# Moving every matmul's two operands to fixed addresses modulo 256 bytes in an AdaLN block with an oscillator scan

## The chip, the cores and the metric

One core of a Trainium2 chip runs the whole program. The metric is device time in microseconds (us), the median of several executions. TensorE (PE in the profile) multiplies, VectorE (DVE), ScalarE (ACT) and GpSimd (POOL) compute beside it, and SyncE issues the transfers. Each of the 128 partitions of the on-chip memory (SBUF) holds the rows of many buffers one behind another; "address" below means the byte offset inside a partition.

## What is computed

Input `x` is [4, 2048, 512] in fp32, with one conditioning row of 512 for each of the four sequences.

```python
mod = silu(c) @ wmod                       # sa, ca, ga, sb, cb, gb
h = layernorm(x) * (1 + ca) + sa
omega, zeta, F = softplus(h @ W_omega), sigmoid(h @ W_zeta), h @ W_B
xs = scan over t of a damped oscillator (64 states z, 64 states y)
x = x + ga * (xs @ C.T + h @ D.T)
h = layernorm(x) * (1 + cb) + sb
xr, xk = mixes of h[t] and h[t-1] by mu_r, mu_k
x = x + gb * sigmoid(xr @ Wr.T) * (relu(xk @ Wk.T)**2 @ Wv.T)
```

## The kernel before

The 8192 rows are worked on as 16 chunks of 512 rows (first layer norm, projections, scan) and 32 units of 256 rows (everything behind the scan). Every fp32 matrix product is made of three float32r products: each operand is split into a high and a low part, and hi·hi, hi·lo and lo·hi are summed in PSUM. `product` (line 328 in the profile) issues them: for each of three passes and each slice `k` of 128 rows of the contraction, `pe.matmul(out, act[a][k], weight[w][k])`. The first operand is the standing one (128 columns, loaded into the array by a LDWEIGHTS, shown as PEld), the second is the moving one (256 or 512 columns). In the profile the moving one is named first: `ps_kr<-wr_hi,mix_r_hi` streams `wr_hi` past a standing `mix_r_hi`. The load for the next matmul runs while the present one streams.

The products of a unit, in this text under one letter each:

- **K** (`k_product`): `mix_k` moves (256 columns), `wk` stands, 48 matmuls, into `ps_kr`
- **R** (`r_product`): `wr` moves (512 columns), `mix_r` stands, 24 matmuls, into `ps_kr`
- **V** (`v_product`): `wv` moves (512), `kk_hi`/`kk_lo` stand, 24 matmuls, into `ps_tv`
- **H** (`h_part`): `wd` moves (512), `h` stands, 24 matmuls, into `ps_cd`
- **S** (`states_part`): `wc` moves (512), `xs_hi`/`xs_lo` stand, 6 matmuls, into `ps_cd`
- **P** (`projections`, once for each chunk): `h` moves (512), `proj` stands, 24 matmuls, into `ps_pt`
- **T1, T2** (lines 336 and 369): transposes of `x_in` and `xn2`, 16 for a chunk and 8 for a unit, `ident` moves (128 columns)

TensorE's order is written out by hand. In the steady part two units make one period: K T2 P R H S V, then K T2 H S T1 R T1 V. Every engine is a queue of its own with semaphores between them. After the residual add, `statistics2` on ScalarE squares both tiles of the unit (`squares`, line 582) and keeps only the row sums; the squares themselves go to a scratch buffer `square_out2` in bf16, and each square waits until the one two before it is done.

Buffers are taken one behind another, each at the next multiple of 32, the first of them at address 1152. Their addresses modulo 256, before and after, as the two lists of `sb(...)` give them:

| product | moving, before | standing, before | moving − standing | moving, after | standing, after | moving − standing |
|---|---|---|---|---|---|---|
| K | mix_k 64 | wk 128 | −64 | 192 | 0 | −64 |
| R | wr 128 | mix_r 64 | +64 | 0 | 64 | −64 |
| V | wv 128 | kk_hi, kk_lo 64 | +64 | 0 | 64 | −64 |
| H | wd 128 | h 128 | 0 | 0 | 64 | −64 |
| S | wc 128 | xs_hi, xs_lo 224 | −96 | 0 | 64 | −64 |
| P | h 128 | proj 128 | 0 | 64 | 128 | −64 |
| T1 | ident 128 | x_in 192 | −64 | 64 | 64 | 0 |
| T2 | ident 128 | xn2 64 | +64 | 64 | 64 | 0 |

All slices of a buffer that a matmul takes start a multiple of 512 bytes from the buffer's start, so a product has the same difference in all its matmuls. (−64 is taken modulo 256, +192 is the same.) Before, `gate_a` and `gate_b` lie at 160, `square_out1` at 96, `xs` at 224; the other large buffers lie at multiples of 64.

Of the kernel before, what the change touches and what calls it, by code (L numbers as in the profile page):

```python
# [7 lines left out]
F32 = mybir.dt.float32  # L8
F32R = mybir.dt.float32r
# [3 lines left out]
B, T, D, M = 4, 2048, 512, 64  # L13
P = 128
KC = D // P
CHUNK, UNIT, HALF = 512, 256, 256
# [3 lines left out]
TPU, TPC = UNIT // P, CHUNK // P  # L20
# [18 lines left out]
def build(nc, d):  # L39
    ctx = ExitStack()  # L40
    with ctx:
        def sb(name, shape, dt=F32):
            return ctx.enter_context(nc.sbuf_tensor(name, shape, dt))

        def sem(name):
            return ctx.enter_context(nc.semaphore(name))


        proj = [sb(f"proj_{n}", [P, KC, 256], F32R) for n in ("hi", "lo")]
        wd = [sb(f"wd_{n}", [P, KC, D], F32R) for n in ("hi", "lo")]  # L50
        wc = [sb(f"wc_{n}", [P, D], F32R) for n in ("hi", "lo")]
        wk = [sb(f"wk_{n}", [P, KC, D], F32R) for n in ("hi", "lo")]
        wr = [sb(f"wr_{n}", [P, KC, D], F32R) for n in ("hi", "lo")]
        wv = [sb(f"wv_{n}", [P, KC, D], F32R) for n in ("hi", "lo")]
        ident = sb("ident", [P, P])
        scan_bias = sb("scan_bias", [P, 4])
        y_bias = sb("y_bias", [P, 1])
# [7 lines left out]
        cb1 = sb("cb1", [P, B, KC])  # L65
        cur_h = sb("cur_h", [P, 2 * KC])
        cur_m = sb("cur_m", [P, NTAB])
        gate_a = sb("gate_a", [P, D])
        gate_b = sb("gate_b", [P, D])
        minus_half = sb("minus_half", [P, TPC])  # L70

        x_in = sb("x_in", [P, TPC, D])
        gate_cols = sb("gate_cols", [P, 3, 2, B * D // P])
        sum1 = sb("sum1", [P, TPC])
        norm_bias1 = sb("norm_bias1", [P, TPC])
# [2 lines left out]
        var1 = sb("var1", [P, TPC])  # L78
        bn_parts = sb("bn_parts", [P, TPC, 6])
        bn = sb("bn", [P, TPC, 2])  # L80
        square_out1 = sb("square_out1", [P, 2, D], mybir.dt.bfloat16)
        square_out2 = sb("square_out2", [P, 2, D], mybir.dt.bfloat16)
        rstd1 = sb("rstd1", [P, TPC])
        h_full = sb("h_full", [P, KC, CHUNK])
        h = [[sb(f"h_{n}{i}", [P, KC, CHUNK], F32R) for n in ("hi", "lo")] for i in range(2)]

        x2 = sb("x2", [P, 4, TPU, D])
        sum2 = sb("sum2", [P, 2, TPU])
        neg_mean2 = sb("neg_mean2", [P, 2, TPU])
        sq2 = sb("sq2", [P, 2, TPU])  # L90
        var2 = sb("var2", [P, 2, TPU])
        rstd2 = sb("rstd2", [P, 2, TPU])
        last_n = sb("last_n", [P, KC])
        mix_full = sb("mix_full", [P, 2, KC, UNIT])
        mix = [mix_full[:, n] for n in range(2)]


        with nc.sbuf_tensor("stage_mix", [P, 2, KC, D], F32) as stage_mix:
            pass
        mixs = [[sb(f"mix_{n}_{w}", [P, KC, UNIT], F32R) for w in ("hi", "lo")] for n in "kr"]  # L100
        with nc.sbuf_tensor("stage_kk", [P, KC, D], F32) as stage_kk:
            pass
        kks = [sb(f"kk_{m}", [P, KC, UNIT], F32R) for m in ("hi", "lo")]
        with nc.sbuf_tensor("stage_out", [P, KC, D], F32) as stage_out:
            pass
        xn2 = sb("xn2", [P, TPU, D])
        rt = sb("rt", [P, TPU, D])
        kk = sb("kk", [P, 2, 2 * UNIT])

        om_pos = sb("om_pos", [P, HALF])  # L110
        om_exp = sb("om_exp", [P, HALF])
        ze = sb("ze", [P, HALF])
# [5 lines left out]
        tmp0 = sb("tmp0", [P, 384])  # L118
        tmp1 = sb("tmp1", [P, 384])
        state = sb("state", [P, 3, HALF + 1])  # L120
        xs = sb("xs", [P, CHUNK])
        xss = [sb(f"xs_{m}", [P, CHUNK], F32R) for m in ("hi", "lo")]


        x2_a, x2_b = (x2[:, i:i + 2].rearrange("p a t n -> p (a t) n") for i in (0, 2))
# [62 lines left out]
        s_mean2, s_sq2, s_var2 = sem("s_mean2"), sem("s_sq2"), sem("s_var2")  # L188
# [379 lines left out]
        def _(act):  # L568
# [8 lines left out]
            def squares(x, neg_mean, scratch, out, count, s_sq):  # L577

                for i in range(out.shape[1]):
                    if count + i >= 2:  # L580
                        act.wait_ge(s_sq, count + i - 1)
                    act.activation(scratch[:, i % 2, :], x[:, i, :], ACT.Square, bias=neg_mean[:, i:i + 1],  # L582
                                   accum_out=out[:, i:i + 1]).then_inc(s_sq, 1)

            def squares1(q):
                act.wait_ge(s_mean1, q + 1)
                squares(x_in, neg_mean1, square_out1, sq1, q * TPC, s_sq1)

            def statistics2(u):
                act.wait_ge(s_x2, u * TPU + TPU)  # L590
                act.activation(neg_mean2[:, u % 2, :], sum2[:, u % 2, :], ACT.Identity, scale=-1.0 / D)\
                   .then_inc(s_mean2, 1)
                act.wait_ge(s_mean2, u + 1)
                squares(x2[:, u % 4], neg_mean2[:, u % 2], square_out2, sq2[:, u % 2], u * TPU, s_sq2)

            def normalise1(q, tiles=range(TPC)):

# [231 lines left out]
            states_out_first()  # L829
            weight_high("wv")  # L830
            statistics2(0)
            omega_out(1)
            shifted(0)
            mix_high(0, 0)
            statistics2(1)
            mix_high(0, 1)
            zeta_and_b_out(1)
# [24 lines left out]
            normalise1(3)  # L862
            h_blocks(3, (0, 1))
            statistics2(2)
            h_high(3, (0, 1))
            shifted(2)
# [688 lines left out]
```

## Time and profile before

| what | value |
|---|---|
| median of 3 runs | 976.93 us (976.89 to 977.65) |
| the profiled execution | 977.14 us, of which the span (first to last instruction) is 975.4 us |
| PE busy | 935.9 us, 96% |
| PE weight loads | 786.9 us, 81% |
| DVE, ACT, POOL busy | 820.9, 691.5, 93.5 us |
| mean granted TensorE clock | 0.981 |

Busy time is the time in which an engine had an instruction of the program in work. Matmuls overlap in the records, so what one costs is read from the distance between the starts of two, not from its own duration. The chain that ended last is followed back from the last instruction to what released it.

### The profile page before, as it was taken

How to read it: one execution, taken by the hardware profiler on the slowest of the kernel's cores; microseconds unless marked ns; L12 is line 12 of the kernel's file. 1: busy time of each engine (PE TensorE's matmuls, PEld its weight loads, DVE VectorE, ACT ScalarE, POOL GpSimd, SP SyncE). 2: the span in 40 equal slices, each digit the busy share in tenths (PEclk: the TensorE clock that was granted, in tenths of full speed). 3: DMA queues.
4: the chain of work that ended last, by engine and by line, in shares of the span. 5: the costliest groups of instructions: out<-in, count | busy, mean ns of one | idle time of the engine just before them, and what ended most of it. 6: DMA issues, size and time to landing. Idle time of an engine off the chain costs nothing.

```text
span 975.4 us, 14746 instructions
## 1 busy us (share of the span) xinstructions
PE 935.9 (96%) x5012; PEld 786.9 (81%) x5012; DVE 820.9 (84%) x2280; ACT 691.5 (71%) x1354; POOL 93.5 (10%) x117
## 2 busy tenths in 40 slices
PE   9995979899999999999999999999999999998997
PEld 3574858788888888888888888888888888887886
DVE  4897779898989989898998979898997989697562
ACT  4979765768777686777868686877768677765451
POOL 0001010001100202010200101110110201000000
PEclk9997998999999999999999999999999999999999
DMA  9820311020211312021121312021131201111001
GB/s 327 280 56 23 109 34 53 12 98 23 87 55 44 99 44 70 18 87 44 57 85 44 98 32 77 23 87 45 44 98 44 98 6 39 44 44 44 23 22 44
DMA packets 35275, 64.78 MB, mean 66 GB/s; under 512 B 3704, under 2 KB 4344, under 8 KB 35200
## 3 DMA queue, kind: packets, MB, share of 16 engines
q1 hardware_dynamic: 35200, 63.84, 19.8%
q8 instruction: 40, 0.66, 0.3%
q14 instruction: 35, 0.29, 0.1%
HBM read 47.02 MB, written 16.81 MB: 65 GB/s over the span
## 4 chain that ended last, share of the span: by engine, by line
PE 83%; DVE 8%; ACT 6%; issue 1%; DMA 1%; DVEq 0%; SPq 0%; ACTq 0%
PE ps_kr L328 32%; PE ps_cd L328 20%; PE ps_tv L328 18%; PE ps_pt L328 7%; PE ps_tv L369 3%; PE ps_pt L336 3%; ACT mix_full L734 1%; DMA stage_out<-in_wd 1%; DVE mix_full L985 1%; PE ps_cd L376 1%; DVE tmp L1206 1%; ACT x_in L600 1%; DVE state L1210 1%; PE ps_tv L389 0%; DVE tmp L1130 0%
## 5 line engine op out<-in xcount | busy, mean ns | idle before, releaser
L985 DVE SCALAR_TENSOR_TENSOR mix_full<-ps_tv,cur_m,mix_full 128x256 f32<-128x256 f32 x256 | 119.1, 479 | 37.7 <-ACT mix_full L734 37.6
L756 ACT ACTIVATE kk<-ps_kr 128x512 f32<-128x512 f32 x64 | 38.1, 599 | 123.4 <-PE ps_kr L328 123.1
L734 ACT ACTIVATE mix_full<-ps_tv,cur_m 128x255 f32<-128x255 f32 x256 | 120.0, 573 | 1.8 <-PE ps_tv L369 1.8
L1484 POOL TENSOR_SCALAR var<-sq 128x2 f32<-128x2 f32 (+1 forms) x34 | 37.1, 1091 | 642.5 <-ACT square_out L582 642.5
L328 PE MATMUL ps_kr<-mix_k_hi,wk_hi 128*128 128x256 f32 x512 | 80.9, 281 | 8.2 <-issue 8.2
L328 PEld LDWEIGHTS ps_kr<-mix_k_hi,wk_hi 128*128 128x128 f32 x512 | 71.2, 191 | 11.2 <-issue 8.8
L328 PE MATMUL ps_kr<-mix_k_hi,wk_lo 128*128 128x256 f32 x512 | 80.1, 279 | 0.0
L328 PE MATMUL ps_kr<-mix_k_lo,wk_hi 128*128 128x256 f32 x512 | 80.0, 279 | 0.0
L328 PE MATMUL ps_kr<-wr_hi,mix_r_hi 128*128 128x512 f32 x256 | 71.5, 402 | 5.5 <-ACT kk L756 5.5
L328 PE MATMUL ps_tv<-wv_hi,kk_hi 128*128 128x512 f32 x256 | 72.8, 408 | 0.8 <-issue 0.8
L328 PE MATMUL ps_kr<-wr_hi,mix_r_lo 128*128 128x512 f32 x256 | 69.9, 395 | 0.0
L328 PE MATMUL ps_tv<-wv_lo,kk_hi 128*128 128x512 f32 x256 | 69.9, 395 | 0.0
L328 PE MATMUL ps_kr<-wr_lo,mix_r_hi 128*128 128x512 f32 x256 | 69.8, 395 | 0.0
L328 PE MATMUL ps_tv<-wv_hi,kk_lo 128*128 128x512 f32 x256 | 69.1, 392 | 0.0
L328 PEld LDWEIGHTS ps_kr<-mix_k_lo,wk_hi 128*128 128x128 f32 x512 | 69.0, 190 | 0.0
L328 PEld LDWEIGHTS ps_kr<-mix_k_hi,wk_lo 128*128 128x128 f32 x512 | 68.6, 190 | 0.0
L328 PE MATMUL ps_cd<-wd_hi,h_hi 128*128 128x512 f32 x248 | 68.1, 396 | 0.0
L328 PE MATMUL ps_cd<-wd_lo,h_hi 128*128 128x512 f32 x248 | 66.4, 390 | 0.0
L328 PE MATMUL ps_cd<-wd_hi,h_lo 128*128 128x512 f32 x248 | 66.4, 389 | 0.0
L748 ACT ACTIVATE mix_k_hi<-mix_full 128x512 fp32r<-128x512 f32 x64 | 40.4, 641 | 33.9 <-DVE mix_full L985 33.6
L328 PEld LDWEIGHTS ps_kr<-wr_hi,mix_r_hi 128*128 128x128 f32 x256 | 47.6, 191 | 15.7 <-issue 5.9
L328 PEld LDWEIGHTS ps_tv<-wv_lo,kk_hi 128*128 128x128 f32 x256 | 49.1, 192 | 11.3
(213 smaller groups left out, 2239.6 us busy)
## 6 DMA issues: line engine op xcount, KB each, us to landing
x<-in_x SPq DMA_DIRECT2D x32, 512.0 KB, 3.7
out<-x SPq DMA_DIRECT2D x32, 512.0 KB, 2.8
x_in<-in_x SPq DMA_DIRECT2D x15, 1024.0 KB, 5.1
x<-in_wmod SPq DMA_DIRECT2D x3, 1024.0 KB, 7.6
mix_full<-in_wmod SPq DMA_DIRECT2D x2, 1024.0 KB, 9.1
x_in<-in_x SPq DMA_DIRECT2D x2, 512.0 KB, 5.7
stage_out<-in_wd SPq DMA_DIRECT2D x1, 1024.0 KB, 10.0
stage_mix<-in_wmod SPq DMA_DIRECT2D x1, 1024.0 KB, 10.5
```

The costliest lines, as they stand in the source:

```text
L328: mm = pe.matmul(out, act[a][k], weight[w][k], start=acc0 and a == 0 and w == 0 and k == 0, stop=acc1 and (a, w) == passes[2] and k == n - 1)
L336: mm = pe.transpose(ps_pt[:, k % 2, i * P:(i + 1) * P], x_in[:, i, k * P:(k + 1) * P], ident[:, :])
L369: mm = pe.transpose(ps_tv[:, k // 2, at:at + P], xn2[:, i, k * P:(k + 1) * P], ident[:, :])
L376: pe.matmul(bank, warm[:, 0:P], warm[:, :], start=True, stop=True)
L600: mm = act.activation(x_in[:, i, :], x_in[:, i, :], ACT.Identity, bias=norm_bias1[:, i:i + 1], scale=rstd1[:, i:i + 1])
L734: mm = act.activation(mix[n][:, k, 1:UNIT], ps_tv[:, j, c * UNIT:(c + 1) * UNIT - 1], ACT.Identity, bias=cur_m[:, SHIFT + k:SHIFT + k + 1] ...
L748: act.activation(mixs[n][0][:, 2 * j:2 * j + 2, :], mix[n][:, 2 * j:2 * j + 2, :], ACT.Identity)\
L756: act.activation(kk[:, i, :], ps_kr[:, i, :], ACT.Relu).then_inc(s_relu, 1)
L985: dve.scalar_tensor_tensor(mix[n][:, k, :], ps_tv[:, j, c * UNIT:(c + 1) * UNIT], cur_m[:, alpha + k:alpha + k + 1], mix[n][:, k, :], ALU. ...
L1206: dve.tensor_tensor(t, node, frm.unsqueeze(1).broadcast_to([P, 2, 3, c]), ALU.mult)\
L1210: dve.tensor_reduce(to[:, 0:2], t.rearrange("p i j c -> p i c j"), mybir.AxisListType.X, ALU.add)\
L1484: pool.tensor_scalar(var[:, :], sq[:, :], 1.0 / D, EPS, ALU.mult, ALU.add).then_inc(s_var, 1)
```

## The change

It is a change of the buffer list and of one scratch operand. Pads (`to_128`, `to_0`, `to_64`, `to_mix_k`, `to_mix_r`) and a new order put each standing and each moving buffer at the addresses of the table; the other large buffers follow them at multiples of 64, and the small ones come last. `square_out2` is gone: the squares of the second layer norm are written in fp32 to `xn2` (to `rt` for unit 1), and the wait before a square stays for the first layer norm alone. The instructions of TensorE, their order and their shapes stay as they are.

```diff
+        sb("to_128", [P, 256])
         proj = [sb(f"proj_{n}", [P, KC, 256], F32R) for n in ("hi", "lo")]
+        sb("to_0", [P, 32])
         wd = [sb(f"wd_{n}", [P, KC, D], F32R) for n in ("hi", "lo")]
         wc = [sb(f"wc_{n}", [P, D], F32R) for n in ("hi", "lo")]
         wk = [sb(f"wk_{n}", [P, KC, D], F32R) for n in ("hi", "lo")]
         wr = [sb(f"wr_{n}", [P, KC, D], F32R) for n in ("hi", "lo")]
         wv = [sb(f"wv_{n}", [P, KC, D], F32R) for n in ("hi", "lo")]
+        sb("to_64", [P, 16])
+        h = [[sb(f"h_{n}{i}", [P, KC, CHUNK], F32R) for n in ("hi", "lo")] for i in range(2)]
+        xss = [sb(f"xs_{m}", [P, CHUNK], F32R) for m in ("hi", "lo")]
...
+        for n in "kr":
+            sb(f"to_mix_{n}", [P, 32])
+            mixs.append([sb(f"mix_{n}_{w}", [P, KC, UNIT], F32R) for w in ("hi", "lo")])
...
+        kks = [sb(f"kk_{m}", [P, KC, UNIT], F32R) for m in ("hi", "lo")]
...
+        xn2 = sb("xn2", [P, TPU, D])
+        rt = sb("rt", [P, TPU, D])
+        kk = sb("kk", [P, 2, 2 * UNIT])
+        x_in = sb("x_in", [P, TPC, D])
+        h_full = sb("h_full", [P, KC, CHUNK])
+        x2 = sb("x2", [P, 4, TPU, D])
+        mix_full = sb("mix_full", [P, 2, KC, UNIT])
...
+        xs = sb("xs", [P, CHUNK])
+        gate_a = sb("gate_a", [P, D])
+        gate_b = sb("gate_b", [P, D])
+        square_out1 = sb("square_out1", [P, 2, D], mybir.dt.bfloat16)
         ident = sb("ident", [P, P])
...
-        square_out2 = sb("square_out2", [P, 2, D], mybir.dt.bfloat16)
...
-                    if count + i >= 2:
+                    if scratch is square_out1 and count + i >= 2:
                         act.wait_ge(s_sq, count + i - 1)
...
-                squares(x2[:, u % 4], neg_mean2[:, u % 2], square_out2, sq2[:, u % 2], u * TPU, s_sq2)
+                squares(x2[:, u % 4], neg_mean2[:, u % 2], rt if u == 1 else xn2, sq2[:, u % 2], u * TPU, s_sq2)
```

## Rows read from the trace of the kernel before

**Rows 1.** The page: busy time of each engine, the chain that ended last.
```profile
PE 935.9 (96%) x5012; PEld 786.9 (81%) x5012; DVE 820.9 (84%) x2280; ACT 691.5 (71%) x1354; POOL 93.5 (10%) x117
...
PE 83%; DVE 8%; ACT 6%; issue 1%; DMA 1%; DVEq 0%; SPq 0%; ACTq 0%
PE ps_kr L328 32%; PE ps_cd L328 20%; PE ps_tv L328 18%; PE ps_pt L328 7%; PE ps_tv L369 3%; PE ps_pt L336 3%; ACT mix_full L734 1%; DMA stage_out<-in_wd 1%; DVE mix_full L985 1%; PE ps_cd L376 1%; DVE tmp L1206 1%; ACT x_in L600 1%; DVE state L1210 1%; PE ps_tv L389 0%; DVE tmp L1130 0%
```

**Rows 2.** Stretches of the span: each engine's busy us (instructions), granted clock.
```profile
200.00:300.00 100.00, 100.00 (x549) 86.29 (x548) 91.00 (x254) 75.50 (x149) 10.98 (x14) 1.00 0.17 56
...
700.00:800.00 100.00, 100.00 (x548) 86.20 (x547) 89.93 (x251) 74.77 (x148) 13.58 (x14) 1.00 0.19 59
...
900.00:976.00 76.00, 68.44 (x364) 58.44 (x364) 39.10 (x78) 29.29 (x61) 2.17 (x4) 0.95 0.08 28
```

**Rows 3.** PE's waits from 177 to 883 us: total, times, longest.
```profile
PE ps_cd L328 <- DVE xs_lo L916: 3.3, 1, 3.3
```

**Rows 4.** The chain that ended last, in order: start us, us, what.
```profile
177.46 2.49 PE ps_cd L328 x6
...
878.40 5.49 PE ps_kr L328 x48
...
883.91 0.47 ACT kk L756
...
900.10 2.90 PE ps_cd L328 x6
...
970.20 0.69 DVE rt L1048
```

**Rows 5.** PE's timeline, three products of one unit: start, us, what, count.
```profile
229.31 1.07 PE L328 MATMUL ps_cd<-wd_hi,h_hi 128*128 128x512 f32 x4
...
234.75 0.39 PE L328 MATMUL ps_cd<-wc_hi,xs_hi 128*128 128x512 f32 x1
...
236.16 1.08 PE L328 MATMUL ps_tv<-wv_hi,kk_hi 128*128 128x512 f32 x4
...
241.66 0.64 PE L328 MATMUL ps_kr<-mix_k_hi,wk_hi 128*128 128x256 f32 x4
```

**Rows 6.** The same timeline just before it.
```profile
212.00 0.64 PE L328 MATMUL ps_kr<-mix_k_hi,wk_hi 128*128 128x256 f32 x4
...
217.47 1.04 PE L369 MATMUL ps_tv<-ident,xn 128*128 128x128 f32 x8
218.26 1.17 PE L328 MATMUL ps_pt<-h_hi,proj_hi 128*128 128x512 f32 x4
...
223.82 1.08 PE L328 MATMUL ps_kr<-wr_hi,mix_r_hi 128*128 128x512 f32 x4
```

**Rows 7.** The same timeline, the other unit of the pair.
```profile
247.92 1.17 PE L328 MATMUL ps_cd<-wd_hi,h_hi 128*128 128x512 f32 x4
...
253.48 0.39 PE L328 MATMUL ps_cd<-wc_hi,xs_hi 128*128 128x512 f32 x1
...
254.88 1.03 PE L336 MATMUL ps_pt<-ident,x_in 128*128 128x128 f32 x8
255.67 1.18 PE L328 MATMUL ps_kr<-wr_hi,mix_r_hi 128*128 128x512 f32 x4
...
261.27 1.04 PE L336 MATMUL ps_pt<-ident,x_in 128*128 128x128 f32 x8
262.06 1.17 PE L328 MATMUL ps_tv<-wv_hi,kk_hi 128*128 128x512 f32 x4
...
267.65 0.52 PE L328 MATMUL ps_kr<-mix_k_hi,wk_hi 128*128 128x256 f32 x3
```

**Rows 8.** Groups by line and shape: count, busy us, mean ns, idle before.
```profile
L369 PE MATMUL ps_tv<-ident,xn 128*128 128x128 f32 x256 | 33.2, 273 | 0.1
...
L582 ACT ACTIVATE square_out<-x,neg_mean 128x512 bf16<-128x512 f32 x64 | 45.7, 715 | 1.2
...
L761 ACT ACTIVATE kk<-kk 128x512 f32<-128x512 f32 x64 | 37.8, 660 | 0.0
```

More of the change, by code:

```diff
@@ L54, in build @@
         wv = [sb(f"wv_{n}", [P, KC, D], F32R) for n in ("hi", "lo")]
+        sb("to_64", [P, 16])
+        h = [[sb(f"h_{n}{i}", [P, KC, CHUNK], F32R) for n in ("hi", "lo")] for i in range(2)]
+        xss = [sb(f"xs_{m}", [P, CHUNK], F32R) for m in ("hi", "lo")]
+        with nc.sbuf_tensor("stage_mix", [P, 2, KC, D], F32) as stage_mix:
+            pass
+        mixs = []
+        for n in "kr":
+            sb(f"to_mix_{n}", [P, 32])
+            mixs.append([sb(f"mix_{n}_{w}", [P, KC, UNIT], F32R) for w in ("hi", "lo")])
+        with nc.sbuf_tensor("stage_kk", [P, KC, D], F32) as stage_kk:
+            pass
+        kks = [sb(f"kk_{m}", [P, KC, UNIT], F32R) for m in ("hi", "lo")]
+        with nc.sbuf_tensor("stage_out", [P, KC, D], F32) as stage_out:
+            pass
+        xn2 = sb("xn2", [P, TPU, D])
[5 more added lines that the diff above has]
+        mix_full = sb("mix_full", [P, 2, KC, UNIT])
+        mix = [mix_full[:, n] for n in range(2)]
+        xs = sb("xs", [P, CHUNK])
+        gate_a = sb("gate_a", [P, D])
+        gate_b = sb("gate_b", [P, D])
+        square_out1 = sb("square_out1", [P, 2, D], mybir.dt.bfloat16)
         ident = sb("ident", [P, P])
@@ L67, in build @@
         cur_m = sb("cur_m", [P, NTAB])
-        gate_a = sb("gate_a", [P, D])
-        gate_b = sb("gate_b", [P, D])
         minus_half = sb("minus_half", [P, TPC])
-        x_in = sb("x_in", [P, TPC, D])
         gate_cols = sb("gate_cols", [P, 3, 2, B * D // P])
@@ L80, in build @@
         bn = sb("bn", [P, TPC, 2])
-        square_out1 = sb("square_out1", [P, 2, D], mybir.dt.bfloat16)
-        square_out2 = sb("square_out2", [P, 2, D], mybir.dt.bfloat16)
         rstd1 = sb("rstd1", [P, TPC])
-        h_full = sb("h_full", [P, KC, CHUNK])
-        h = [[sb(f"h_{n}{i}", [P, KC, CHUNK], F32R) for n in ("hi", "lo")] for i in range(2)]
-        x2 = sb("x2", [P, 4, TPU, D])
         sum2 = sb("sum2", [P, 2, TPU])
@@ L93, in build @@
         last_n = sb("last_n", [P, KC])
[L94 to L108, printed above, removed]
         om_pos = sb("om_pos", [P, HALF])
@@ L120, in build @@
         state = sb("state", [P, 3, HALF + 1])
-        xs = sb("xs", [P, CHUNK])
-        xss = [sb(f"xs_{m}", [P, CHUNK], F32R) for m in ("hi", "lo")]
         x2_a, x2_b = (x2[:, i:i + 2].rearrange("p a t n -> p (a t) n") for i in (0, 2))
```

## The prediction

> **What bounds the kernel now.** I read the page first, then the stretches, PE's waits, the chain, and last PE's timeline, which carries the argument. PE is busy 96% of the span, and 83% of the chain that ended last is its [rows 1]. That average hides two kinds of stretch. From 200 to 800 us PE is busy in every microsecond at the full clock (granted 1.00, the 2.4 GHz level) while DVE stands at 90% and ACT at 75% [rows 2]. Between 177 and 883 us PE waits for another engine once, 3.3 us [rows 3], and that wait ends where the stretch begins, with the S at 177.46 [rows 4]. The chain says the same: from 177.46 to 883.91 us it is PE's alone, then it runs over ACT and DVE (the shifted mixes and the end of the last scan) to 900.10, and then again over PE, at a mean granted clock of 0.95 [rows 2], to 970.20 [rows 4]. So a nanosecond saved in a matmul is a nanosecond of the span for 706 + 70 us, and worth nothing in the first 177 us, where other engines and transfers end the waits, nor from 884 to 900 us.
>
> What is a matmul worth there? The distance of starts says it. I take one period of two units, from one K at 212.00 us to that of two units later at 267.65 [rows 6, 7]: 55.65 us. The blocks in it, start to start, beside the difference moving − standing that they have before:
>
> - H behind R: 229.31 to 234.75, 5.44 us for 24 matmuls of 512 columns, 226.7 ns each [rows 5]; difference 0.
> - R behind P: 223.82 to 229.31, 5.49 us [rows 5, 6]; V behind S: 236.16 to 241.66, 5.50 us [rows 5]; the same 24 x 512 columns, difference +64.
> - H behind T2: 247.92 to 253.48, 5.56 us; P behind T2: 218.26 to 223.82, 5.56 us; both 0. R behind T1: 255.67 to 261.27, 5.60 us; V behind T1: 262.06 to 267.65, 5.59 us; both +64 [rows 6, 7]. (The first start behind a transpose is shown early, so these four stand only beside each other.)
> - S: 234.75 to 236.16 and 253.48 to 254.88, 1.41 and 1.40 us for 6 matmuls [rows 5, 7]; at H's rate they would be 1.36; difference −96.
> - K: 212.00 to 217.47, 5.47 us for 48 matmuls of 256 columns, the columns of an H [rows 6]; difference −64.
>
> The reader is to see that products of the same shape don't run at the same rate, with no wait between, and that the rate goes with the difference: 0 has the best one, −64 at 256 columns is within 0.03 us of it, +64 is about 0.04 us a product slower, −96 about 0.045 for only six matmuls.
>
> **The change, part by part.** *R and V, +64 to −64.* If −64 is as good at 512 columns as K shows it at 256, R and V fall to the rate of their neighbours at 0. A period then gains 5.49 − 5.44 = 0.05, 5.50 − 5.44 = 0.06, 5.60 − 5.56 = 0.04 and 5.59 − 5.56 = 0.03: together 0.18 us. The bound on the other side is nothing.
>
> *S, −96 to −64.* H behind R shows that a product can follow another without loss, so I take S at H's rate: 0.05 + 0.04 = 0.09 us a period. If what S loses is the price of starting anew, it is 0.
>
> *H and P, 0 to −64.* Here the difference leaves the value that has the best rate. By K, the only row at −64, it costs nothing: K's 0.03 us over H's is the most that can be put down to it. I take 0. Against that stands that no 512-column product at −64 is in the trace; its bounds are below, under the rivals.
>
> *K* keeps its difference: 0. *T1 and T2* get 0 in place of −64 and +64: a block of 8 takes 0.79 us at either (217.47 to 218.26, 254.88 to 255.67, 261.27 to 262.06) [rows 6, 7], so the difference doesn't matter to them.
>
> *The squares.* 64 squares of 715 ns go from a bf16 to an fp32 output [rows 8]. The nearest row with an fp32 output is the square of `kk`, 660 ns, so ScalarE may save up to 0.06 us each, 64 x 0.055 = 3.5 us of work that lies beside PE (ACT 75% busy); were it as much dearer it would still be hidden by the quarter of ACT's time that is idle. The wait that goes asks for the square two before, done long since: 0. No new wait comes, since `xn2` is free between the residual add, whose sum the statistics wait for, and the normalisation, which waits for the squares. *The other buffers* (gates, `xs`) are operands of DVE and ACT, 90% and 75% busy behind a PE that never waits for them in the long stretch: 0.
>
> *The sum.* A period gains 0.18 + 0.09 = 0.27 us of 55.65. The stretch from 177.46 to 883.91 holds 706.45 / 55.65 = 12.7 periods: 3.43 us. Behind 900.10 us, where S of unit 30 starts, the written order holds three R (units 29 to 31), four V (28 to 31) and two S: 7 x 0.045 + 2 x 0.045 = 0.40 us. Together 3.8 us. What the products before 177 us gain goes into the waits around them: 0. The profiled execution took 977.14 us, 1.7 more than its span and 0.2 more than the median of the runs; 977.14 − 3.8 = 973.3, and from the median 976.93 − 3.8 = 973.1. I give 973.2. A measurement of this kernel can tell about 0.2% (2 us) from nothing. The own range of this case is 972.3 (K's 0.03 goes too) to 974.6 (R and V alone, 0.18 x 12.7 + 7 x 0.045 = 2.6 us, and a rounding).
>
> **A rule that speaks against it.** The rows just shown have 226.7 ns for a matmul at 0 and 5.50 / 24 = 229.2 ns at +64. The Trainium skill, "TensorE: Matmul & The Clock Gate", Part 2, says in the step on LDWEIGHTS that PE has two independent SBUF read ports, so that loading the next weights doesn't take read bandwidth from the running matmul. By it no distance between the operands could matter and the time would stay at 976.9; that case is the first rival. The trace doesn't agree with it to the letter, by 2.5 ns a matmul.
>
> **The rivals.** *The difference is not the cause (no change).* R and V differ from H in more than the addresses: they stand on `mix_r` and `kk`, written shortly before, and fill other banks. If one of these makes the 0.04 us, nothing falls away: 976.9. The same time comes out if +64 and −64 are alike at 512 columns: R and V stay, H and P lose 3 x 0.045 = 0.135 us a period, and S gains 0.09 less 12 x 0.0019 = 0.07, which leaves 0.065 x 12.7 = +0.8 us, 977.7. For it: nothing in the trace separates the sides of 64 at 512 columns. Against it: K at −64 runs at H's rate, and H, too, stands on a buffer just written.
>
> *More falls away.* The period has 7 x 5.44 + 2 x 5.44 + 2 x 1.36 = 51.68 us of products at H's rate, and 32 transposes, of which a block of 8 shows (1.04 − 0.273) / 7 = 0.11 us each [rows 6, 8]: 3.5 us, 55.2 in all. The rest is 0.47 us, of which my sum takes 0.27. What is left, about 0.2 us, is K behind V and four products behind transposes. If equal differences take that away too, the gain is 0.47 x 12.7 + 0.7 = 6.7 us: 970.2. Against it: H and P lose it at difference 0, K at the −64 that all will have.
>
> *Slower: −64 hurts at 512 columns.* S at −96 is the nearest 512-column row on that side: (1.405 − 1.36) / 6 = 7.5 ns a matmul. If H, P, R and V all paid that, a period of 168 such matmuls would get 168 x 0.0075 = 1.26 us, less the 0.18 that R and V pay now: +1.08 x 12.7 = 13.7, and about 1.1 behind 900 us: 991.7. It decides from 0.27 / 168 = 1.6 ns a matmul on: if those products run at over 228.3 ns each, the kernel is slower than before. Against it: K would have to show it, and its matmuls are 5.47 / 48 = 114 ns, half of 228.
>
> **How the numbers follow.** Forecast 0.62, no change 0.17, more falls away 0.11, slower 0.10 (most of that near the point from which it decides, not at its end). For the signs the first and third give faster, 0.73, less a little for a gain under 2 us: 0.71; same 0.20; slower by over 2 us 0.09. For the range I take in the third rival's 970.2 and the second's end of no change: 970.0 to 977.4. That leaves out the slower case and the tail of the others.
>
> **What the profile after will show.** R behind P and V behind S take 5.44 to 5.46 us, R and V behind T1 5.56; S 1.36 to 1.38; H, P and K as before; the period 55.38 us; the distance from one stretch's start at about 177 us to its end about 3.4 us shorter; ACT's squares at about 660 ns, without effect. The first step is wrong if R and V stay at 5.49; the third if H behind R is over 5.44. The prediction as a whole fails if the waits of PE before 177 or from 884 to 900 us move by more than a microsecond for another reason, as an order of ready times there that the new squares shift.

## The result, and the profile after

The changed kernel takes 987.76 us (987.28 to 988.23, 4 runs), the kernel before 977.27 us on the same chip (4 runs): a ratio of 1.0106, 95% interval 1.0093 to 1.0118. It is slower by 10.5 us where I had forecast 3.8 us faster. Its profiled span is 985.5 us, 10.1 more than before. Four later executions, three of the kernel before and one of run 5, took 1341 to 2412 us in a slower state and are left out of all medians.

First the page of the changed kernel, its busy times and its chain. Then one stretch of 100 us, PE's waits from 177 to 893 us, and the two ends of the stretch in which PE alone makes the chain:

```profile
PE 945.4 (96%) x5012; PEld 783.7 (80%) x5012; DVE 822.7 (83%) x2280; ACT 691.2 (70%) x1354; POOL 85.5 (9%) x117
...
PE 84%; DVE 8%; ACT 5%; issue 1%; DMA 1%; SPq 0%; DVEq 0%; ACTq 0%
```

```profile
700.00:800.00 100.00, 100.00 (x541) 84.84 (x540) 89.30 (x256) 74.65 (x147) 10.01 (x12) 1.00 0.21 69
```

```profile
PE ps_cd L334 <- DVE xs_lo L923: 2.9, 1, 2.9
```

```profile
178.72 1.83 PE ps_cd L334 x6
...
894.56 0.47 ACT kk L763
```

The bound has not moved: PE is busy in all 715.84 us of that stretch at the full clock (granted 1.00), and waits once, at its start, as before [rows 2, 3]. The stretch runs from 178.72 to 894.56 us, 715.84 us for 706.45 [rows 4]. So 9.4 of the 10.1 us were lost in a place where PE waits for nobody. Of the rest, the stretch starts 1.3 us later than before (178.72 for 177.46), and what lies behind its end takes about 0.5 us less. PE has the same 5012 matmuls, and they follow each other more slowly. Its timeline over one period of two units, the first row of each block:

```profile
213.61 0.63 PE L334 MATMUL ps_kr<-mix_k_hi,wk_hi 128*128 128x256 f32 x4
...
219.07 1.04 PE L375 MATMUL ps_tv<-ident,xn 128*128 128x128 f32 x8
219.86 1.18 PE L334 MATMUL ps_pt<-h_hi,proj_hi 128*128 128x512 f32 x4
...
225.55 1.09 PE L334 MATMUL ps_kr<-wr_hi,mix_r_hi 128*128 128x512 f32 x4
...
231.15 1.09 PE L334 MATMUL ps_cd<-wd_hi,h_hi 128*128 128x512 f32 x4
...
236.75 0.39 PE L334 MATMUL ps_cd<-wc_hi,xs_hi 128*128 128x512 f32 x1
...
238.15 1.09 PE L334 MATMUL ps_tv<-wv_hi,kk_hi 128*128 128x512 f32 x4
...
243.75 0.63 PE L334 MATMUL ps_kr<-mix_k_hi,wk_hi 128*128 128x256 f32 x4
...
249.20 1.04 PE L375 MATMUL ps_tv<-ident,xn 128*128 128x128 f32 x8
250.00 1.18 PE L334 MATMUL ps_cd<-wd_hi,h_hi 128*128 128x512 f32 x4
...
255.68 0.39 PE L334 MATMUL ps_cd<-wc_hi,xs_hi 128*128 128x512 f32 x1
...
257.08 1.03 PE L342 MATMUL ps_pt<-ident,x_in 128*128 128x128 f32 x8
257.87 1.18 PE L334 MATMUL ps_kr<-wr_hi,mix_r_hi 128*128 128x512 f32 x4
...
263.55 1.03 PE L342 MATMUL ps_pt<-ident,x_in 128*128 128x128 f32 x8
264.34 1.18 PE L334 MATMUL ps_tv<-wv_hi,kk_hi 128*128 128x512 f32 x4
...
270.03 0.63 PE L334 MATMUL ps_kr<-mix_k_hi,wk_hi 128*128 128x256 f32 x4
```

Start to start, beside the same blocks of before [rows 5, 6, 7]:

| block | difference before, after | before, us | after, us |
|---|---|---|---|
| K behind V | −64, −64 | 5.47 | 5.46 |
| P behind T2 | 0, −64 | 5.56 | 5.69 |
| R behind P | +64, −64 | 5.49 | 5.60 |
| H behind R | 0, −64 | 5.44 | 5.60 |
| S | −96, −64 | 1.41, 1.40 | 1.40, 1.40 |
| V behind S | +64, −64 | 5.50 | 5.60 |
| H behind T2 | 0, −64 | 5.56 | 5.68 |
| R behind T1 | +64, −64 | 5.60 | 5.68 |
| V behind T1 | +64, −64 | 5.59 | 5.69 |
| period of two units | | 55.65 | 56.42 |

Every long product with 512 moving columns that does not follow a transpose now takes 5.60 / 24 = 233.3 ns a matmul, for 226.7 at 0 and 229 at +64. K, with 256 columns, keeps its rate. 0.77 us a period times 12.7 periods is 9.8 us.

The squares, in fp32 to `xn2`, take what they took in bf16 [rows 8]; the group of the changed kernel (count, busy us, mean ns, idle before):

```profile
L588 ACT ACTIVATE xn<-x,neg_mean 128x512 f32<-128x512 f32 x62 | 44.4, 717 | 1.0
```

### The profile page after: what moved, and what is told of

It reads as the page before. It is cut to its first block, busy times and chain, and to the rows that moved or that the text cites. A ratio compares the mean times of both kernels' runs of the same rounds, so it can differ in the third digit from the quotient of the medians.

```text
span 985.5 us, 14715 instructions
## 1 busy us (share of the span) xinstructions
PE 945.4 (96%) x5012; PEld 783.7 (80%) x5012; DVE 822.7 (83%) x2280; ACT 691.2 (70%) x1354; POOL 85.5 (9%) x117
## 4 chain that ended last, share of the span: by engine, by line
PE 84%; DVE 8%; ACT 5%; issue 1%; DMA 1%; SPq 0%; DVEq 0%; ACTq 0%
PE ps_kr L334 32%; PE ps_cd L334 20%; PE ps_tv L334 18%; PE ps_pt L334 8%; PE ps_tv L375 3%; PE ps_pt L342 2%; ACT mix_full L741 1%; DVE mix_full L992 1%; DMA x<-in_wmod 1%; PE ps_tv L395 1%; DVE tmp L1213 1%; ACT x_in L607 1%; DVE state L1217 0%; DVE tmp L1137 0%; DVE tmp L1157 0%
## 5 line engine op out<-in xcount | busy, mean ns | idle before, releaser
L1491 POOL TENSOR_SCALAR var<-sq 128x2 f32<-128x2 f32 (+1 forms) x34 | 32.6, 959 | 652.6 <-ACT xn L588 601.4
L334 PE MATMUL ps_cd<-wd_hi,h_hi 128*128 128x512 f32 x248 | 70.2, 405 | 0.0
L334 PE MATMUL ps_cd<-wd_lo,h_hi 128*128 128x512 f32 x248 | 68.7, 399 | 0.0
```

The lines of the kernel that those rows point to most:

```text
L334: mm = pe.matmul(out, act[a][k], weight[w][k], start=acc0 and a == 0 and w == 0 and k == 0, stop=acc1 and (a, w) == passes[2] and k == n - 1)
L1491: pool.tensor_scalar(var[:, :], sq[:, :], 1.0 / D, EPS, ALU.mult, ALU.add).then_inc(s_var, 1)
```

## The experiments

All kernels but run 7 are variants of the changed one in which only the pads are set anew, unless the diff says otherwise. The diffs are excerpts: some show one pad for several, and the words behind a # are mine and not in the kernels. Pads are given in fp32 elements, 64 of them are 256 bytes. "−64" and the like is moving − standing modulo 256, as in the table ahead of the prediction. The period of two units is read as above, K to K. Runs 2, 3, 4, 8, 10, 11 and 12 were executed once each: they are read product by product in the trace, not by their times.

**1. All differences 0.**

```diff
-        sb("to_128", [P, 256])
-        sb("to_0", [P, 32])
-        sb("to_64", [P, 16])
-            sb(f"to_mix_{n}", [P, 32])
```

> All pads taken out of the changed kernel, so that every buffer of a product starts at 128 modulo 256 and every product (K, R, V, H, S, P) has the difference 0; the squares go to xn2 as in the changed kernel. Theory 1 (the rate of a 512-column matmul goes with the difference moving minus standing): R, V and S fall to the rate that H had before, 226.7 ns a matmul, so R behind P and V behind S 5.44 us, S 1.36 to 1.40, K 5.47, a period of two units 55.4 us, and the time 973 us, about 4 under the kernel before and 14.5 under the changed one. Rival 1 (the squares in fp32, or the new places of the other buffers, slow TensorE's reads): the matmuls stay at 233 ns, a period 56.4 us, 988 us. Rival 2 (R and V differ from H by their role, not their address): R and V stay at 229 ns or above, a period of 55.55 us or more, 976 to 977 us.

981.05 us, ratio 1.0034 (1.0021 to 1.0046). PE's timeline:

```profile
224.09 1.07 PE L332 MATMUL ps_kr<-wr_hi,mix_r_hi 128*128 128x512 f32 x4
...
229.53 1.07 PE L332 MATMUL ps_cd<-wd_hi,h_hi 128*128 128x512 f32 x4
...
234.97 0.39 PE L332 MATMUL ps_cd<-wc_hi,xs_hi 128*128 128x512 f32 x1
...
236.33 1.07 PE L332 MATMUL ps_tv<-wv_hi,kk_hi 128*128 128x512 f32 x4
...
241.77 0.64 PE L332 MATMUL ps_kr<-mix_k_hi,wk_hi 128*128 128x256 f32 x4
...
247.53 1.04 PE L373 MATMUL ps_tv<-ident,xn 128*128 128x128 f32 x8
```

R, H and V take 5.44 us each (224.09, 229.53, 234.97; 236.33 to 241.77), S 1.36. So R and V are not slow by their role, and the squares and the new places of the other buffers slow nothing: both rivals fall, and the gain that I had forecast for R, V and S is there: without what K loses, the period is 0.29 us shorter, for 0.27 forecast. But K takes 5.76 us (241.77 to 247.53) for 5.47: at 0, the best difference of 512 columns, 256 columns run at 120 ns a matmul (5.76 / 48). Two K cost 0.57 us a period, more than the rest gains: 55.93 us. Theory 1 was right for 512 columns and wrong in keeping K at 5.47 us, and with it in the 973 us.

**2 and 3. A map of differences.** Pads so that each product has a difference of its own, then dealt out anew.

```diff
 # run 2: wd..wv 0, proj 128, h 160, xs 0, mix_k 0, mix_r 128, kk 32
+        sb("pad_wd", [P, 32])
+        sb("pad_h", [P, 40])
+        sb("pad_xs", [P, 24])
...
+            sb("pad_mix_r", [P, 32])
...
+        sb("pad_kk", [P, 40])
...
 # run 3: wd..wv 0, proj 160, h 32, xs 192, mix_k 128, mix_r 224, kk 160
```

> The pads of the changed kernel set so that each product has another difference moving minus standing: P +32, H +96, R 128, V -32, S 0, K 0. It is read product by product. Theory 1: S at 226.7 to 230 ns, K 113.3; the other values are not in any trace so far; by nearness to known ones, P between 226.7 and 229.5 (between 0 and +64), V between 226.7 and 233.3 (between 0 and -64), H and R unknown, 226.7 to 233.3. Rival 2 (by role or by place, not by difference): H, P, R and V all as in the changed kernel, 233 ns.

> As the run before with the differences dealt out anew: P 128, H -32, R +32, V +96, S +64, K 128. Theory 1: each 512-column difference gives the rate that it gave in the run before to another product, within 1 ns (H as V there, R as P there, V as H there, P as R there); S at +64 at 229 to 231 ns. Rival 2: the rates stay with the products and do not move with the differences.

994.87 and 993.78 us (the kernel before beside them 977.73). Run 2's timeline, R, H, S, V and K:

```profile
226.08 1.09 PE L337 MATMUL ps_kr<-wr_hi,mix_r_hi 128*128 128x512 f32 x4
...
231.68 1.09 PE L337 MATMUL ps_cd<-wd_hi,h_hi 128*128 128x512 f32 x4
...
237.27 0.40 PE L337 MATMUL ps_cd<-wc_hi,xs_hi 128*128 128x512 f32 x1
...
238.66 1.09 PE L337 MATMUL ps_tv<-wv_hi,kk_hi 128*128 128x512 f32 x4
...
244.25 0.63 PE L337 MATMUL ps_kr<-mix_k_hi,wk_hi 128*128 128x256 f32 x4
...
250.00 1.03 PE L378 MATMUL ps_tv<-ident,xn 128*128 128x128 f32 x8
```

R at 128 takes 5.60 us, H at +96 5.59, V at −32 5.59. In run 3, R at +32, H at −32 and V at +96 take 5.59, 5.59 and 5.60. The rate is the same whichever product has the difference, which is what Theory 1 said. That +32 would lie between 0 and +64 was wrong: it is as slow as −64, and −32 too is at the top of the range given for it. K at 0 takes 5.75 here, and 5.70 and 5.76 at 128. S, behind a slow H, takes 1.39 at 0 and at +64.

**4. The same differences, 64 bytes further on.**

```diff
-        sb("to_128", [P, 256])
+        sb("pad_proj", [P, 16])   # proj 192, wd..wv 64, h, xs, mix_r, kk 128, mix_k 0
...
```

> All differences at -64 as in the changed kernel, but every operand 64 bytes further on: weights at 64, h, mix_r, kk and xs halves at 128, proj 192, mix_k 0. Theory 1: only the difference counts, so all rates are those of the changed kernel (233.3 ns at 512 columns, K behind V 5.46 us, a period 56.42 us), 987 to 988 us. Rival 3 (the absolute place of the moving operand modulo 256 counts: at 128 it was fast in H and P before): the rates change with the shift by more than 1 ns a matmul, 975 to 1000 us.

987.8 us; H 5.60, V 5.60, R 5.59, K 5.46 (but for the first of the long stretch, 5.66). Rival 3 falls: with every operand 64 bytes further on and the same differences, no product's time moves by more than 0.01 us.

**5. 512 columns at 0, K at −64.**

```diff
-        for n in "kr":
-            sb(f"to_mix_{n}", [P, 32])
+        for n, gap in (("k", 48), ("r", 16)):
+            sb(f"pad_mix_{n}", [P, gap])   # mix_k 64, all others 128
```

> Every product with a 512-column moving operand (P, H, S, R, V) at difference 0, K (256 columns) at -64: weights, h, proj, mix_r, kk and the xs halves at 128 modulo 256, mix_k at 64. Theory 4 (the best difference depends on the columns of the moving operand: 0 at 512, -64 at 256, and the products do not act on each other): R behind P, V behind S and H behind R 5.44 us, S 1.36, K 5.46, a period of two units 55.33 us, 973 us, 0.4% under the kernel before. Rival 5 (the sum of all stalls of a period is conserved, they only move: what K lost at 0 was what R, V and S had gained): a period of 55.6 us, 977 us.

977.91 us, ratio 1.0009 (1.0000 to 1.0018): not the 973 of Theory 4. It is near the 977 of Rival 5, but a conserved sum of stalls does not fit the periods, which go from 55.46 us (run 14) to 56.42. All 512-column products run at 0's rate. V does so although its pads put `kk` 256 bytes further from `wv` than in run 1 (5.44 us in both), which fits a count modulo 256. But K does not come back. Its first row and that of T2 behind it:

```profile
212.43 0.63 PE L332 MATMUL ps_kr<-mix_k_hi,wk_hi 128*128 128x256 f32 x4
...
218.09 1.04 PE L373 MATMUL ps_tv<-ident,xn 128*128 128x128 f32 x8
```

5.66 us at the very addresses modulo 256 (64 and 128) at which it takes 5.47 in the kernel before. The kernel before, late in the span, has this rate as well:

```profile
909.32 0.63 PE L328 MATMUL ps_kr<-mix_k_hi,wk_hi 128*128 128x256 f32 x4
...
914.98 1.03 PE L369 MATMUL ps_tv<-ident,xn 128*128 128x128 f32 x8
...
933.74 0.64 PE L328 MATMUL ps_kr<-mix_k_hi,wk_hi 128*128 128x256 f32 x4
...
939.21 1.04 PE L369 MATMUL ps_tv<-ident,xn 128*128 128x128 f32 x8
```

909.32 to 914.98 is 5.66 us, 933.74 to 939.21 is 5.47, one kernel, one layout. K at −64 has two rates, 5.66 / 48 = 117.9 and 5.47 / 48 = 114.0 ns as a block's mean. Matmul by matmul, the trace of the kernel before has 117 to 120 ns from start to start through the slow K at 909.32. In a fast one it has up to five distances of 116 to 123 ns and then 113 or 114, up to the last. Every K of the long stretch is a fast one there.

**6. H and P alone back at 0.**

```diff
-        sb("to_128", [P, 256])
-        sb("to_0", [P, 32])
+        sb("pad_proj", [P, 32])   # proj 0, wd..wv 0
-        sb("to_64", [P, 16])      # h 0
+        sb("pad_xs", [P, 16])     # xs 64, the others as in the changed kernel
```

> The changed kernel with H and P alone put back to difference 0 (weights, h and proj at 0 modulo 256), the others at -64. Theory 4: H behind R 5.44 us for 5.60, H and P behind transposes 5.55 for 5.69, the others unchanged, so a period of 56.42 - 0.16 - 0.13 - 0.13 = 56.0 us and 982.5 us: half of what the change lost comes back. Rival 1 (something else of the change slows all): H and P stay at 233 ns, 988 us.

984.89 us, ratio 1.0081 (1.0068 to 1.0094): 2.9 us of the 10.5 come back, about 5 were expected. R and H of its timeline:

```profile
224.50 1.09 PE L334 MATMUL ps_kr<-wr_hi,mix_r_hi 128*128 128x512 f32 x4
...
230.10 1.09 PE L334 MATMUL ps_cd<-wd_hi,h_hi 128*128 128x512 f32 x4
...
235.57 0.40 PE L334 MATMUL ps_cd<-wc_hi,xs_hi 128*128 128x512 f32 x1
```

H is back at 5.47 (230.10 to 235.57), 0.03 us over what it takes behind an R at 0, P at 5.56, R stays at 5.60. Most of the missing part is K's: one K of each pair takes 5.65 us, the other 5.46, so the period is 56.23 and not 56.0.

**7. The squares alone.** The kernel before with the two edited lines of `squares` and `statistics2` and no other change.

> The kernel before with the squares' edit alone: fp32 squares into xn2 (rt for unit 1), no wait between the squares of the second layer norm, all addresses as before. Theory 4: no product changes, squares about 660 ns in place of 715, time within 0.5 us of the kernel before, 977 to 978 us. Rival 1: a matmul rate changes or ScalarE's lateness moves a wait, over 2 us either way.

977.21 us, ratio 1.0000 (0.9991 to 1.0009). The squares take 716 ns, not 660: bf16 or fp32 as the output's type makes no difference here (715 and 716 ns), and the edit is worth nothing.

**8 and 10. P in halves of 256 columns**, at 0 (otherwise as run 5) and at −64.

```diff
-                    product(ps_pt[:, m, :], ..., [[h_q[w][:, k, :] ...]]).then_inc(s_p, 1)
+                    for t in (slice(0, 256), slice(256, 512)):
+                        mm = product(ps_pt[:, m, t], ..., [[h_q[w][:, k, t] ...]])
+                    mm.then_inc(s_p, 1)
```

> As the run with 512 columns at 0 and K at -64, but P issued as two halves of 256 columns (48 matmuls with h moving, same products, same sums), still at difference 0. Theory 4: it is the column count, not the role, that makes K slow at 0: P's matmuls take 120 ns as K's did at 0, P 5.76 us or more for 5.44, about 0.3 us a chunk, 977 to 978 us. Rival 6 (K is slow at 0 for another reason, its buffers or its bank): P at 113.3 ns a half, the time unchanged.

> 512-column products at 0 except P, which is issued as two halves of 256 columns at -64; K at +64. Theory 5: P's halves take 113.3 or 117.8 ns, as K does at -64, and not the 120 of the run with P's halves at 0; K at +64 is not in any trace, between 113.3 and 120. Rival 6 (the role decides, not the column count): P's halves stay at 120.

The first row of P and the first of R behind it, at 0:

```profile
218.59 0.72 PE L332 MATMUL ps_pt<-h_hi,proj_hi 128*128 128x256 f32 x4
...
224.43 1.09 PE L332 MATMUL ps_kr<-wr_hi,mix_r_hi 128*128 128x512 f32 x4
```

and at −64:

```profile
218.26 0.72 PE L334 MATMUL ps_pt<-h_hi,proj_hi 128*128 128x256 f32 x4
...
223.80 1.09 PE L334 MATMUL ps_kr<-wr_hi,mix_r_hi 128*128 128x512 f32 x4
```

5.84 us at 0, 5.54 at −64, for the same columns that an undivided P takes in 5.56 us at 0 (kernel before) and in 5.69 at −64 (changed kernel). So the order of 0 and −64 turns round with the column count, in one and the same product: it is the count, not K. The times are 981.23 and 977.69 us. 977 to 978 was expected for the first, on the assumption that run 5 would take 973; against run 5's 977.9 the 0.29 us more in each of 12.7 periods fit. K at +64 in the second takes 5.66.

**9. V back at +64.** `mix_k` and `kk` at 64, all others at 128.

> As the run with 512 columns at 0 and K at -64, but V alone back at +64, as in the kernel before. Theory 5 (K at -64 has two rates, 113.3 and 117.8 ns, and which one it takes depends on the matmuls in front of it: behind a V at +64 or -64 it falls into the fast one, behind a V at 0 it does not): V behind S 5.50 us and behind T1 5.59, K 5.47 again, all others as in the run at 0, a period of 55.45 us and 974.5 us, 0.25% under the kernel before. Rival 7 (K's slow rate comes from the layout itself, its pads or its buffers' place above 256 bytes): K stays at 5.66, a period 55.8 us, 979 us.

977.66 us, ratio 1.0006 (0.9997 to 1.0015), where 974.5 was expected. In the long stretch K takes 5.66 and 5.47 in turn: slow behind the V that follows S, fast behind the V that follows T1. Towards the end it is the other way round (the K at 909.91 us, behind S and V, is fast, the one at 934.03 slow). Rival 7 falls, since one layout gives both. K's buffers lie at the very addresses of run 5, and everything behind `kk` was moved by 256 bytes in all, so V's difference is what changed, and with it half of the K. Theory 5 is right in that, but V's difference alone does not decide.

**11 and 12. K at −32 and +32**, P at −96 in the first, all 512 columns otherwise at 0.

> 512-column products at 0 except P at -96; K at -32. Theory 5: P at 233.3 ns like every 512-column product that is neither at 0 nor at +64; K at -32 between 113.3 and 120, unknown. H, R, V, S stay at 226.7. Rival: the products share a state, so that P's rate drags R, which follows it, for more than a few matmuls.

> All 512-column products at 0, K at +32. Theory 5: K at 117 to 120 ns, since every difference tried at 256 columns but -64 gave that; a period of 55.7 to 55.95 us, 979 to 982 us. If it is 113.3 ns instead, K behind a V at 0 has a fast difference and the period is 55.3 us, 973 us.

K takes 5.68 us at −32 and 5.60 at +32 (116.7 ns, a little under the 117 to 120 expected). P at −96 takes 5.70 behind T2, a slow product like those at −64, and the R behind it 5.48 for the 5.44 that it takes behind a P at 0. 979.98 and 976.01 us, the second for 979 to 982 expected.

**13 and 14. Only `kk_lo` moved**, the standing operand of eight of V's matmuls, the last four among them; K at −64, all else at 0.

```diff
-        kks = [sb(f"kk_{m}", [P, KC, UNIT], F32R) for m in ("hi", "lo")]
+        kks = [sb("kk_hi", [P, KC, UNIT], F32R)]
+        sb("pad_kk_lo", [P, 16])   # run 13: kk_lo 192, V lo at -64; run 14: 48, kk_lo 64, V lo at +64
+        kks.append(sb("kk_lo", [P, KC, UNIT], F32R))
```

> As the run with 512 columns at 0 and K at -64, with kk_lo alone moved 64 bytes on: of V's 24 matmuls the 8 that stand on kk_lo, the last four before K among them, are at -64, the other 16 at 0. Theory 5 (the state in which V leaves the array decides K's rate): K falls into 113.4 ns, 5.46 us, as it does behind a V wholly at -64; V costs 8 x 6.6 = 0.05 us more, 5.49 behind S; a period of 55.45 us for 55.74, 974.5 us, 0.25% under the kernel before. Rival 7 (K's slow rate comes with the layout): K stays at 5.66, a period of 55.85 us, 980 us.

> The same with kk_lo 64 bytes back, so that those 8 matmuls of V are at +64. Theory 5: V costs 8 x 2.3 = 0.02 us more; K takes 113.8 or 117.8 ns, perhaps in turn, as it did behind a V at +64; a period of 55.4 us if always fast, 55.6 if in turn, 55.8 if never: 974 to 979 us. Rival 7: K at 5.66 in every unit.

Run 13: 981.13 us, ratio 1.0041 (1.0027 to 1.0055). V costs 0.08 us more behind S (5.52 for 5.44), not 0.05: in the trace the first four matmuls at −64 take 229 to 236 ns, and so do the next six, which are at 0 again. K stays slow in every unit:

```profile
242.24 0.63 PE L334 MATMUL ps_kr<-mix_k_hi,wk_hi 128*128 128x256 f32 x4
...
247.90 1.04 PE L375 MATMUL ps_tv<-ident,xn 128*128 128x128 f32 x8
```

That is a miss of Theory 5 as I had put it. Run 14: **973.88 us, ratio 0.9970 (0.9958 to 0.9982)**, the only version that beats both kernels. K, T2, and then V, K, T2 of its timeline:

```profile
211.17 0.63 PE L334 MATMUL ps_kr<-mix_k_hi,wk_hi 128*128 128x256 f32 x4
...
216.64 1.04 PE L375 MATMUL ps_tv<-ident,xn 128*128 128x128 f32 x8
...
235.25 1.07 PE L334 MATMUL ps_tv<-wv_hi,kk_hi 128*128 128x512 f32 x4
...
240.73 0.63 PE L334 MATMUL ps_kr<-mix_k_hi,wk_hi 128*128 128x256 f32 x4
...
246.19 1.04 PE L375 MATMUL ps_tv<-ident,xn 128*128 128x128 f32 x8
```

V behind S takes 5.48 us, and every K from 185 to 935 us takes 5.46 or 5.47; the period is 55.46 us. K's own buffers lie where they lay in run 5, and K went from 5.66 to 5.46. This pair is less clean than run 9, though: with `kk_lo` everything behind it in the list moved too (`xn2`, `x_in`, the gates and others, by −64 modulo 256 in run 14 and by +64 in run 13), and no run moves these alone.

**15. K at +32 again, timed.**

> The kernel with all 512-column products at 0 and K at +32 again, now timed: K at 116.7 ns, 5.605 us, in every unit, a period of 55.61 us for 55.65 before, so 0.5 us faster than before, between 0.1% faster and no difference. Theory 5 expects no second rate of K here, since none was seen.

976.64 us, ratio 0.9996 (0.9987 to 1.0005), K at 5.60 or 5.61 through the long stretch: no difference from the kernel before.

**Which K is fast.** The starts of single matmuls in the traces say more. Take the distance from the start of V's last matmul to the start of K's first, in ns, for every K at −64 and the full clock behind 180 us, in all ten kernels that have such a K (before, changed, runs 4 to 9, 13 and 14):

| V's last distance | K behind it | of these fast |
|---|---|---|
| 226 to 229 ns | 106 | 0 |
| 230 ns | 15 | 8 |
| 231 to 236 ns | 157 | 157 |

A V at 0 (runs 5 and 8) goes on at 226 or 227 to its last matmul, and all K behind it are slow. A V at +64 runs in a beat of about 226, 229 and 232 ns: in the kernel before it ends on 230 or 231 through the long stretch (the first one on 236), and the one slow K, at 909.32 us, is behind a V that ends on 227. In run 9's long stretch it ends on 226 or 227 behind S and on 230 or 231 behind T1. Run 13's V ends on 229 or 230, run 14's on 235 or 236. So, but for those at 230 ns, one distance sorts the K of runs 6, 9, 13 and 14, which V's difference does not. It is a correlation over 278 K, found when all runs were made: no run sets that distance by itself, and it may be a sign of the cause and not the cause.

The period accounts for the times to within 1 us. Worked out is its difference from 55.65 us, times 12.7; measured is the difference from the kernel before, in us:

| run | period, us | worked out | measured |
|---|---|---|---|
| changed | 56.42 | +9.8 | +10.5 |
| 1, all at 0 | 55.93 | +3.6 | +3.3 |
| 5, 512 at 0, K −64 | 55.74 | +1.1 | +0.7 |
| 6, H and P at 0 | 56.23 | +7.4 | +7.6 |
| 9, V at +64 | 55.69 | +0.5 | +0.8 |
| 13, V lo at −64 | 55.93 | +3.6 | +4.0 |
| 14, V lo at +64 | 55.46 | −2.4 | −3.2 |
| 15, K at +32 | 55.61 | −0.5 | −0.5 |

## Why the prediction was wrong

- *What bounds the kernel* was right: what the period gained or lost between 177 and 884 us came out in the time, to within 1 us in the eight kernels of the table.
- *R and V, +64 to −64* is the step that failed, and *H and P, 0 to −64* with it. Both carry K's row over to another column count, the first in the words "If −64 is as good at 512 columns as K shows it at 256", the second by "K, the only row at −64". It is not as good: 233.3 ns at 512 columns, in every product and at either place (changed kernel, run 4). R and V lost 0.11, 0.10, 0.08 and 0.10 us where I gave them 0.05, 0.06, 0.04 and 0.03 of gain; H and P lost 0.16, 0.12 and 0.13 where I gave 0. The prediction itself had noted that no 512-column product at −64 was in the trace. It then gave the only row at that difference, which has another shape, more weight than the 512-column row nearest to it, S at −96.
- *S, −96 to −64*: 0.01 us for 0.09. −96 and −64 are both slow differences. At 0, where run 1 put it, S does take the 1.36 us.
- *K keeps its difference: 0* held in size (5.46 for 5.47), but not for the reason given: its rate is not fixed by its difference (5.47 and 5.66 in one kernel), so that it held was in part luck.
- *T1 and T2* and the *other buffers*: nothing, as said. *The squares*: nothing for the time (run 7), but no 0.06 us each either.
- *The first 177 us: 0* was short by 1.3 us: the long stretch starts at 178.72 us for 177.46. That is more than the microsecond that the prediction had set as its own limit there, and no run isolates why. Behind 900 us, where the 512-column matmuls are slower too, the changed kernel took about 0.5 us less: from the start of the first S there to that of the next K it took 8.48 us for 9.22, at a mean granted clock of 0.82 for 0.74.
- *The slower rival* was the right mechanism, with a chance of 0.10. Its price was 7.5 ns a matmul from S at −96, and its time 991.7 us; measured were 6.6 ns and 987.8 us. The point from which it decides, 228.3 ns, was passed by 5 ns. The argument against it, that K would have to show it, was false.
- *The difference is not the cause* fell in run 1: R and V at 0 run at H's rate. So the forecast gain of R, V and S, 0.27 us a period, exists, but at 0 and not at −64, and only as long as K is not slowed in turn.
- *The rule of two independent read ports* (the Trainium skill, "TensorE: Matmul & The Clock Gate", Part 2) would have every 512-column row of the map alike. The runs do not agree with it: they have 226.7 to 233.3 ns at 512 columns by the difference alone. What stays open is where inside the chip the two reads meet, and the runs do not show that the weight load's read is the one that collides; they show that the distance of the two operands matters.

Open is also why K has two rates at −64. Shown is that it is not K's layout (runs 5, 9 and 14 have K's buffers at the same addresses) and that a change of V's difference, in run 9, changes half of the K. V's difference alone is no rule: behind a V at −64 every K from 187 to 944 us was fast in the changed kernel and about every other one in run 6, which differs from it in H and P. What they go with is V's last distance in the table above, but not shown is what sets it, nor that it is the cause.

## What to carry to other kernels

Read a matmul's cost from start to start, product by product, and when products of one shape differ with no wait between, compare their operands' addresses modulo 256; here the difference is worth 3% of a matmul. Do not carry the rate of one column count over to another: what was best for 256 columns was among the worst for 512. And when a layout is tuned, time the whole order, since a product's rate can change with the one ahead of it: K's did, by 0.19 us of 5.47.

## What the runs showed of the hardware

The rate of a float32r matmul at the full clock by moving − standing, in ns, from blocks start to start (5.54, 5.70 and 5.84 us are behind T2 and stand only beside others there):

| difference | 512 columns | 256 columns |
|---|---|---|
| 0 | 226.7 (H, R, V) | 120 (K, 5.76 us; P in halves 5.84 us) |
| +32 | 233 (R) | 117 (K, 5.60 us) |
| +64 | 229 (R, V) | 118 (K, 5.66 us) |
| +96 | 233 (H, V) | not tried |
| 128 | 233 (R) | 119 or 120 (K, 5.70 or 5.76 us) |
| −96 | slow (P 5.70 us, S 1.41) | not tried |
| −64 | 233.3 (H, R, V) | 114 or 118 (K, 5.47 or 5.66 us; P in halves 5.54 us) |
| −32 | 233 (H, V) | 118 (K, 5.68 us) |

Transposes of 128 columns showed no such effect: 0.79 us a block of 8 at −64, 0 and +64. A change of difference leaves a trace in what follows: at difference 0, H takes 5.47 us behind an R at −64 and 5.44 behind one at 0 (runs 6 and 5). That a stream of matmuls has two stable rates at one layout, and that which of them it takes goes with the last distance of the stream ahead, I had not expected at all.
